# Packed tile counts in registers and an earlier first tile, in the expert stage of an adaLN block

## The reference

```python
probs = softmax(x @ gate_weight.T);  top_p, sel = top_k(probs, 2);  top_p /= sum(top_p) + 1e-8
out = swiglu(x, shared)                               # inner size 938
for e in range(8):
    out += cw[..., e] * swiglu(x, experts[e])         # cw is top_p where e was picked, else 0
x = x + gb * out
```

## Time and profile before

| | us |
|---|---|
| median of 3 runs | 783.69 (783.38 to 783.82) |
| the profiled execution's own time | 781.73 |
| its span (the trace runs from 0 to 779.9) | 779.9 |
| attention, router, shared expert | 0 to 398.5 |
| expert stage, turn of tile 0 to the turn behind tile 18 | 398.52 to 740.61 |
| last results, final sum and output | 740.61 to 779.9 |

### The profile page before, as it was taken

How to read it: one execution, slowest core, us unless ns; L and a number is a source line. 1 busy time by engine, 2 the same in 40 slices (tenths; PEclk the granted TensorE clock), 3 DMA queues, 4 the chain that set the end, 5 groups by cost and what they waited for, 6 DMA issues and landing times.

```text
span 779.9 us, 12016 instructions
## 1 busy us (share of the span) xinstructions
PE 669.7 (86%) x3026; PEld 503.3 (65%) x3027; DVE 561.2 (72%) x1230; ACT 431.6 (55%) x822; POOL 375.4 (48%) x299
## 2 busy tenths in 40 slices
PE   4768989899899989897789998999999998999910
PEld 1546767677666766674557776777677776777700
DVE  4878969889797979985647665666666675766637
ACT  4457566675757656653445554555555565555600
POOL 1323654647384554636318291836154172922145
PEclk9598979999998989989799999999999999999965
DMA  8303000000000000010310322313103103110046
GB/s 257 90 1 96 28 27 19 10 30 24 27 27 27 27 12 28 14 34 22 116 49 6 128 65 82 92 41 116 39 17 116 41 4 116 43 34 21 27 139 194
DMA packets 41297, 44.55 MB, mean 57 GB/s; under 512 B 8052, under 2 KB 31976, under 8 KB 41280
## 3 DMA queue, kind: packets, MB, share of 16 engines
q1 hardware_dynamic: 36672, 35.88, 15.6%
q0 software_dynamic: 4608, 8.47, 3.3%
HBM read 31.61 MB, written 13.76 MB: 58 GB/s over the span
## 4 chain that ended last, share of the span: by engine, by line
PE 37%; DVE 27%; issue 16%; POOL 11%; DMA 3%; SPq 2%; ACT 2%; POOLq 1%; DVEq 1%; ACTq 0%
PE PS L603 33%; POOL w_lo L434 4%; PE PS L606 4%; DVE acc L1268 3%; POOL w_hi L429 3%; DVE al L1255 3%; DVE prod L1248 2%; SPq L306 2%; DMA xin<-sorted_dram 1%; POOL pair L489 1%; DVE yT L1358 1%; DVE wd L1341 1%; POOL result_dram L562 1%; DVE PS L1248 1%; POOL sorted_dram L499 1%
## 5 line engine op out<-in xcount | busy, mean ns | idle before, releaser
L961 ACT ACTIVATE sg<-PS 128x512 f32<-128x512 f32 x216 | 128.7, 596 | 150.1 <-PE PS L603 148.8
L603 PE MATMUL PS<-xh,w_lo 128*128 128x512 f32 x405 | 177.2, 438 | 15.8 <-issue 7.1
L1248 DVE TENSOR_TENSOR PS<-PS,sg 128x512 f32<-128x512 f32 (+1 forms) x160 | 111.3, 697 | 109.1 <-PE PS L603 98.3
L562 POOL DMA_INDIRECT result_dram<-y_rows,aux_d x80 | 78.0, 975 | 186.7 <-DVE y_rows L1620 156.1
L603 PE MATMUL PS<-xh,w_hi 128*128 128x512 f32 x405 | 162.9, 402 | 0.0
L603 PE MATMUL PS<-xl,w_hi 128*128 128x512 f32 x405 | 162.8, 402 | 0.0
L499 POOL DMA_INDIRECT sorted_dram<-h,slot x64 | 74.0, 1156 | 90.0 <-DVE slot L1455 64.1
L603 PEld LDWEIGHTS PS<-xh,w_lo 128*128 128x128 f32 x405 | 78.3, 193 | 48.8 <-DVE prod L1248 13.5
L1255 DVE TENSOR_TENSOR al<-PS,ah 128x512 fp32r<-128x512 f32 x140 | 95.5, 682 | 7.7 <-ACT ah L969 5.0
L603 PE MATMUL PS<-ah,w_lo 128*128 128x512 f32 x216 | 96.5, 447 | 3.8 <-ACT ah L969 3.8
L969 ACT CAST ah<-PS 128x512 fp32r<-128x512 f32 (+1 forms) x160 | 92.8, 580 | 8.5 <-DVE PS L1248 8.1
(11 more groups left out here) (223 smaller groups left out, 1114.9 us busy)
## 6 DMA issues: line engine op xcount, KB each, us to landing
stage<-in_w_gu SPq DMA_DIRECT2D x18, 448.0 KB
xin<-sorted_dram SPq DMA_DIRECT2D x20, 260.0 KB, 2.7
stage<-in_w_dn SPq DMA_DIRECT2D x9, 448.0 KB
tab<-mods_dram SPq DMA_DIRECT2D x8, 384.0 KB, 3.6
sorted_dram<-pad SPq DMA_DIRECT2D x8, 260.0 KB, 2.4
out<-X SPq DMA_DIRECT2D x4, 512.0 KB, 3.2
stage<-result_dram SPq DMA_DIRECT2D x3, 512.0 KB, 5.2
result_dram<-y_rows,aux_d POOLq DMA_INDIRECT x80, 2.2
```

Of the source, the lines that this page charges most:

```text
L562: pool.indirect_dma_start(out=result_dram, out_offset=bass.IndirectOffsetOnAxis(ap=aux_d[:, r:r + 1].bitcast(U32), axis=0), in_=y_rows[:, ...
L603: return nc.tensor.matmul(out, lhsT, rhs, start=start, stop=stop, **k)
L961: A.activation(dst, src, ACT.Silu).then_inc(s["silu_done"], 1)
L1248: V.tensor_tensor(product_in(where, c)[0:n, :], bank("up", where, c)[0:n, :], sg[0:n, c % 3, :], ALU.mult).then_inc(s["prod_done"], 1)
```

## The change

Constants get one more row, `digit` = 8^e for e = 0 to 7. Behind the plan VectorE makes one integer out of the eight counts, sum over e of (count - 1) * 8^e. TensorE loads it once and takes the counts out with register arithmetic; its expert stage is written out for all 8 experts. SyncE asks for the first tile of expert e + 1 as the last load of expert e's loop, and pads expert e + 1 at the start of expert e.

```diff
+MAX_TILES = TOKENS // TILE
+    digit = MAX_TILES ** np.arange(E)[None, :] + 0 * u
@@ VectorE, behind the plan and ahead of product(g, 1, WIDE)
             V.tensor_copy(plan[:, 0:2, :], plan_f[:, 0:2, :]).then_inc(s["plan_ready"], 1)
             V.engine_nop().then_inc(s["aux_read"], 1)
+            link(V.scalar_tensor_tensor(plan_f[:, 3, :], plan_f[:, 0, :], -1.0, S["digit"], ALU.add, ALU.mult))
+            link(V.tensor_reduce(word_f[:], plan_f[:, 3, :], AX.X, ALU.add))
+            V.tensor_copy(word[:], word_f[:]).then_inc(s["word_ready"], 1)
             product(g, 1, WIDE)
@@ TensorE
-            def expert(e, buf, first=None):
-                if first is None:
-                    tiles, first = tiles_of(pe, e)
-                else:
-                    tiles = tile_count(pe, e)
+            pe.wait_ge(s["word_ready"], 1)
+            digits = pe.value_load(word[0:1, 0:1], min_val=0, max_val=MAX_TILES ** E - 1)
+            bits = MAX_TILES.bit_length() - 1
...
+            pe.reg_mov(left, digits)
+            pe.reg_mov(done, 0)
+            for e in range(E):
+                pe.reg_alu(here, left, MAX_TILES - 1, ALU.bitwise_and)
+                pe.reg_add(here, here, 1)
+                tiles = pe.snap(here, min_val=1, max_val=MAX_TILES)
+                first = pe.snap(done, min_val=0, max_val=MAX_FIRST)
                 pe.wait_ge(s["split_done"], e + 2)
                 apart(pe)
                 with pe.Fori(0, tiles) as t:
-                    tile_body(buf, first + t)
-                return first + tiles
-
-            with pe.Fori(0, E // 2 - 1) as k:
-                expert(2 * k + 1, 0, expert(2 * k, 1))
-            count = expert(E - 1, 0, expert(E - 2, 1))
+                    tile_body((e + 1) % 2, first + t)
+                pe.reg_add(done, done, here)
+                pe.reg_alu(left, left, bits, ALU.logical_shift_right)
@@ SyncE
             def expert(e):
                 tiles, first = tiles_of(sp, e)
-                sp.wait_ge(s["pads_out"], 16 * (e + 1))
-                apart(sp)
+                if e + 1 < E:
+                    pad_rows(e + 1)
+                    sp.wait_ge(s["pads_out"], 16 * (e + 2))
                 with sp.Fori(0, tiles) as t:
-                    load_tile(e * REGION + t * TILE, first + t)
+                    sp.reg_alu(row, t, 1, ALU.add)
+                    sp.reg_alu(keep, row, tiles, ALU.not_equal)
+                    sp.reg_alu(last, row, tiles, ALU.is_equal)
...                                        # row = e * REGION + (t + 1) * TILE, or (e + 1) * REGION at the last t
+                    load_tile(sp.snap(row, min_val=0, max_val=(E - 1) * REGION + TOKENS), first + t + 1)
                 return first + tiles

-            with sp.Fori(0, E - 2) as e:
-                expert(e)
-                pad_rows(e + 1)
-                sp.wait_ge(s["split_done"], e + 3)
-                load_raw(e + 3)
-            expert(E - 2)
-            pad_rows(E - 1)
-            count = expert(E - 1)
-            load_tile(0, count)
+            sp.wait_ge(s["pads_out"], 16)
+            load_tile(0, 0)
+            for e in range(E):
+                count = expert(e)
+                if e + 2 < E:
+                    sp.wait_ge(s["split_done"], e + 3)
+                    load_raw(e + 3)
```

More of the change, by code:

```diff
@@ L96, in constants @@
     many = np.arange(E)[None, :] * TILE + 0 * u
-    small = np.concatenate([upto, equal, block, *roles, seg, E - expert, expert * REGION, many], 1)
+    digit = MAX_TILES ** np.arange(E)[None, :] + 0 * u
+    small = np.concatenate([upto, equal, block, *roles, seg, E - expert, expert * REGION, many, digit], 1)
     big = np.concatenate([np.broadcast_to(m, (P, P)) for m in mats], 1)
@@ L106 @@
 for _name, _n in (("upto", BLK), ("equal", BLK), ("block", NB), ("upper", 9), ("lower", 9), ("seg", E * GC),
-                  ("rev", E), ("region", E), ("many", E)):
+                  ("rev", E), ("region", E), ("many", E), ("digit", E)):
     SMALL[_name] = (_at, _n)
@@ L209, in adaln_block @@
         cmp = sb("cmp", [P, E, E])
+        word_f = sb("word_f", [P, 1])
+        word = sb("word", [P, 1], I32)
         pad = sb("pad", [P, TR, ROW])
@@ L269, in adaln_block @@
             ah_ready al_ready al_late down_done y_bank_done y_sb_ready yt_done y_out gated_free tile_in xt_done rh_ready
-            rl_ready aux_read aux_moved results_out plan_ready pads_out final_added final_gated final_sum final_ready_dve final_ready_pool
+            rl_ready aux_read aux_moved results_out plan_ready word_ready pads_out final_added final_gated final_sum final_ready_dve final_ready_pool
             out_done gb_in""".split()
@@ L286, in adaln_block @@
         NRAW = 7
-        MAX_TILES = TOKENS // TILE
         MAX_FIRST = 2 * TOKENS // TILE + E
@@ L386, in load_tile @@
                     s["tile_in"], 16)
+            last = sp.alloc_register("last_tile")
+            keep = sp.alloc_register("not_last")
+            row = sp.alloc_register("next_row")
             def expert(e):
                 tiles, first = tiles_of(sp, e)
-                sp.wait_ge(s["pads_out"], 16 * (e + 1))
-                apart(sp)
+                if e + 1 < E:
+                    pad_rows(e + 1)
+                    sp.wait_ge(s["pads_out"], 16 * (e + 2))
                 with sp.Fori(0, tiles) as t:
-                    load_tile(e * REGION + t * TILE, first + t)
-                return first + tiles
-            with sp.Fori(0, E - 2) as e:
-                expert(e)
-                pad_rows(e + 1)
-                sp.wait_ge(s["split_done"], e + 3)
-                load_raw(e + 3)
-            expert(E - 2)
-            pad_rows(E - 1)
-            count = expert(E - 1)
-            load_tile(0, count)
+                    sp.reg_alu(row, t, 1, ALU.add)
+                    sp.reg_alu(keep, row, tiles, ALU.not_equal)
+                    sp.reg_alu(last, row, tiles, ALU.is_equal)
+                    sp.reg_alu(row, row, keep, ALU.mult)
+                    sp.reg_alu(row, row, TILE, ALU.mult)
+                    sp.reg_alu(row, row, e * REGION, ALU.add)
+                    if e + 1 < E:
+                        sp.reg_alu(last, last, REGION, ALU.mult)
+                        sp.reg_alu(row, row, last, ALU.add)
+                    load_tile(sp.snap(row, min_val=0, max_val=(E - 1) * REGION + TOKENS), first + t + 1)
+                return first + tiles
+            sp.wait_ge(s["pads_out"], 16)
[5 more added lines that the diff above has]
+                    load_raw(e + 3)
             sp.wait_ge(s["results_out"], 64 * (count + 1))
@@ L927, in tile_body @@
                 down(buf, I, FC - 1, WIDE)
-            def expert(e, buf, first=None):
-                if first is None:
-                    tiles, first = tiles_of(pe, e)
-                else:
-                    tiles = tile_count(pe, e)
+            pe.wait_ge(s["word_ready"], 1)
+            digits = pe.value_load(word[0:1, 0:1], min_val=0, max_val=MAX_TILES ** E - 1)
+            bits = MAX_TILES.bit_length() - 1
+            left = pe.alloc_register("tiles_left")
+            here = pe.alloc_register("tiles_here")
+            done = pe.alloc_register("tiles_done")
+            pe.reg_mov(left, digits)
[5 more added lines that the diff above has]
+                first = pe.snap(done, min_val=0, max_val=MAX_FIRST)
                 pe.wait_ge(s["split_done"], e + 2)
@@ L936, in expert @@
                 with pe.Fori(0, tiles) as t:
-                    tile_body(buf, first + t)
-                return first + tiles
-            with pe.Fori(0, E // 2 - 1) as k:
-                expert(2 * k + 1, 0, expert(2 * k, 1))
-            count = expert(E - 1, 0, expert(E - 2, 1))
+                    tile_body((e + 1) % 2, first + t)
+                pe.reg_add(done, done, here)
+                pe.reg_alu(left, left, bits, ALU.logical_shift_right)
+            count = pe.snap(done, min_val=1, max_val=MAX_FIRST)
             pe.wait_ge(s["rl_ready"], count + 1)
```

## The result

The changed kernel takes 773.61 us, median of 4 runs (770.41 to 778.39), against 783.76 before: ratio 0.9853, 95% interval 0.9809 to 0.9897. Both say 10 us; 7.7 were forecast. Executions of one kernel lie up to 10 us apart, most of the long ones at a lower granted clock, while the stage that the change touches repeats better in the traces; so what follows is read from the stage. The profiled execution went from 781.73 to 773.72, its span from 779.9 to 771.9.

A forecast was written before the change was run, and what follows sets the result against it. TensorE, busy 86% of the span, was taken as the bound, its stage losing 15.3 us to waits. Terms 4.6 + 0.6 - 0.5 + 2.0 + 1.0 gave 7.7 us off 783.69, so 776.0 us, range 772.5 to 778.5.

The forecast's parts named there:

- Registers: TensorE at expert openings: register steps replace value loads of the counts, gaining 4.6 us, ends 2.0 and 7.4.
- the 1.2 that I took off for lost cover: Openings of experts 1, 2, 3 and 6: register work no longer starts behind an `xin` wait, costing 1.2 us.
- the gain ahead of that: TensorE's expert boundaries: 1.6 us from those with one load plus 4.2 from those with two, 5.8 us.
- The earlier tile: SyncE loads the next tile ahead of raw weights: 4.4 us of waits go, 2.4 return, gaining 2.0 us.
- The forecast losses at tiles 2, 4, 6 and 14: Waits for late result rows after the `xin` waits go: 0.55, 0.68, 0.14 and 1.1 us.
- Three-tile experts: Tiles 8 and 11: raw loads move one tile on, result rows land sooner, gaining 1.0 us, ends 0 and 1.0.
- First tile: TensorE's start of tile 0: two value loads become one, the other can't be hidden; gain 0.6 us.
- The word: VectorE's three small operations ahead of `product(g, 1)` delay TensorE, costing 0.5 us, ends 0.3 and 0.8.
- Rival A: Result rows take back the whole wait for `xin`: gain 5.7 us, time 778.0 us; chance 0.17.
- Rival B: TensorE's six register operations cost as much as the load replaced, 0.8 us: sum 4.8, 778.9 us; chance 0.11.
- Rival C: Fetching TensorE's four extra written-out bodies stalls it 2.7 us each, 10.8 us: 786.8 us; chance 0.07.

The follow-up runs named there:

- e2: The changed kernel with the old SyncE order, so only the word and TensorE's registers: stage 337.67 us, ratio 0.9945 to the kernel before.
- e6: e4 with zero to four useless extra value loads of the word on TensorE per expert: stage 341.22 us, ratio 1.0007 to the kernel before.
- e9: The changed kernel timed again with no edit: 773.54 us, stage 333.07 us, ratio 0.9869 to the kernel before.
- e4: The changed kernel with SyncE's raw weight loads waiting until the result rows have landed: 769.99 us, stage 330.57 us, ratio 0.9812 to the kernel before.
- e7: e4 with TensorE's stage written out for these inputs' 19 tiles, reading no counts: stage 328.53 us, ratio 0.9803 to the kernel before.
- e1: The kernel before with only SyncE's part of the change, TensorE keeping its value loads: stage 343.89 us, ratio 0.9989 to the kernel before.
- e5: e1 with raw weight loads waiting until the result rows have landed: stage 337.46 us, ratio 0.9964 to the kernel before.
- e10: The same program as e8, run again: 770.53 us, stage 330.34 us, ratio 0.9823 to the kernel before.
- e8: e4 with the word made later by VectorE and read by TensorE ahead of the first turn: 768.84 us, stage 330.20 us, ratio 0.9824.

## Why the prediction was right, term by term

- **Registers, forecast 4.6.** Openings went from 7.4 to 2.2 without the late rows: 5.2. The unpacking was sized right (0.4 against 0.35), and so was the 1.2 that I took off for lost cover: e2, with the cover in place, gains 6.4, and without it 5.2 are left. Too small was the gain ahead of that, 5.8 against e2's 6.4. The boundaries with one load came out at 1.7 where 1.6 stood, and expert 6's, with two loads, at 1.2. Experts 2 and 4 gained 1.7 each, not 1.4: they also lose the pair loop, which the sum had at some 0.2 each. TensorE's sequencer before, at expert 2:

```profile
L940 PEldq ALU_OP  x1: 36/36/36, 473.2 to 473.2; - x1
L940 PEldq COMPARE_BRANCH  x1: 214/214/214, 473.3 to 473.3; - x1
L940 PEldq FUSED_REGOPS  x1: 59/59/59, 473.6 to 473.6; - x1
```

That is 0.45 us, 473.2 to 473.65. The 0.8 of sequencer time of a load shows as 0.7 on TensorE (e6).
- **The earlier tile, forecast 2.0.** All four waits went, 1.7 of 4.4 came back, 2.7 are left. The forecast losses at tiles 2, 4, 6 and 14 were 0.55, 0.68, 0.14 and 1.1; measured, over 0.31, 0.53, 0.09, 0.00 and 1.12. Three are right, tile 4's failed: `aux_w` came 19.83 us behind the split's start (451.40 to 471.23), not 20.48. That is luck of this execution: in the repeat (e9) the tile lost 0.3 there. That it is the raw loads which hold the rows up in these tiles, e4 shows.
- **Three-tile experts, forecast 1.0:** tiles 8 and 11 at 17.23 and 17.24, 0.95. **First tile, forecast 0.6:** 19.44 to 18.86, 0.58. The other load is partly hidden behind the cast of `xh`, though, which the forecast ruled out: no more than 0.4 us of load and unpacking shows, against e7. **The word, forecast -0.5:** 3.22 to 3.69 of idle, -0.47.
- **The sum** is 5.2 + 2.7 + 0.95 + 0.58 - 0.47 = 9.0 where 7.7 stood; the timed medians say 10, and the interval of the ratio is 7 us wide, so the last 1 us is not explained. No luck of opposite errors is in it: the two terms that are off, 0.6 and 0.7, both gained more than was forecast.
- **What I had wrong in kind:** I added the two parts as if each were worth its own term. For the earlier tile by itself these terms gave 339 to 340 (the expectation of e1), and 343.89 came. Rival A, rows that take back the whole wait for `xin`, is what happens with the value loads and the late rows both in place (e1: 4.3 of 4.4 us came back, and 3.2 for the clock). Taking either away makes the earlier tile pay: the registers, which take the sequencer's work out from behind the last `al` (5.2, from e2 to the change), or rows that land sooner (4.5, e5). The sum was for the whole change, where the two don't meet, and so this did not touch it.
- **Rival B** is refuted by three steps in 0.4 us and by openings of experts 4 and 7 near 17.5. **Rival C**: the profile's instruction queue q8 has 10 packets where it had 7, and the windows show nothing for it; with 19 bodies (e7) it has 16, and the openings are 17.19 to 17.24. The rule of the Trainium skill that I set beside it, in "Runtime: NRT & Kernel Launch", section Instruction fetch mechanics, holds here as far as straight code goes. Its 200 ns for a register load is short of the price: the load itself is 304 ns, and e6 measures 0.7 us with the steps around it.

## What to carry to other kernels

Two stalls at one place can be in series through the sequencer: taking the data wait away moved the register work behind a later semaphore, and the stall was there almost in full (e1). Before removing a wait, look for what else runs in its shadow and whether that starts at the wait's end or at another event. And a gap behind a transfer may be one of contention: one wait that kept the bulk load off four small writes brought 2 us of stage (e4), at no cost to the split that wanted the load.

## What the runs showed of the hardware

A value load costs TensorE 0.7 us at each use, when nothing covers it, for an instruction of 0.3 (e6). The granted clock after an idle time did not follow its length: it fell behind 2.08 and 1.66 us (e1) and 2.03 (e6), and stayed at the full level behind 1.72 (e1) and 2.81 (e6). In the first tile it was down in e10 and up in e8, with the same program and 0.73 us of idle before the first matmul in both. One such fall costs 1.5 to 1.6 us, a third of what the earlier tile and the raw loads together are worth here.
